# Moving the first input-gate matmul behind the last block of layer 1

## The reference

```python
xn = layernorm(x)
# attention branch (Di = 512, K = 64, R = 16)
u     = xn @ up_w.T                                   # [T, Di]
shift = silu(causal_conv4(u) + conv_b)
v     = sigmoid(u @ ig_w1.T @ ig_w2.T + ig_b2) * u    # the input gate
q, k  = shift @ q_w.T, shift @ k_w.T
g     = softplus(shift @ g_w.T + g_b);  tau = sigmoid(shift @ tau_w.T + tau_b)
o     = gla_chunk_scan(q, k_normed * g**tau, v, -g * tau)
o     = rmsnorm((o + shift * residual_weight) * silu(xn @ gate_w.T)) @ down_w.T
# feed-forward branch (D_HID = 1024, ternary weights with a scale per output)
h = silu(w1(xn)) * w2(xn)                             # layer 1
h = gelu(h1(h)); h = gelu(h2(h)); y = w3(h)
out = x + o + y
```

## Time and profile before

| | us |
|---|---|
| median of 3 runs | 2048.26 (2047.7 to 2049.34) |
| profiled execution, its own time | 2048.48 |
| span of the profiled execution | 2046.7 |
| TensorE busy in it | 1989.6 (97%) |
| VectorE busy | 1576.1 (77%) |
| ScalarE busy | 1260.1 (62%) |

### The profile page before, as it was taken

How to read it: one execution, slowest core, us unless ns; L and a number is a source line. 1 busy time by engine, 2 the same in 40 slices (tenths; PEclk the granted TensorE clock), 3 DMA queues, 4 the chain that set the end, 5 groups by cost and what they waited for, 6 DMA issues and landing times.

```text
span 2046.7 us, 46221 instructions
## 1 busy us (share of the span) xinstructions
PE 1989.6 (97%) x17218; PEld 1966.2 (96%) x17218; DVE 1576.1 (77%) x4242; ACT 1260.1 (62%) x2495; POOL 68.5 (3%) x104
## 2 busy tenths in 40 slices
PE   0999999999999999999999999999999999999998
PEld 0999999999999999999999999999999999999998
DVE  7777778877777877787777788777778777878776
ACT  5665656666566666566656566665566665666564
POOL 0000000000000000000000000000000000000000
PEclk9999999999999999999999999999999999999999
DMA  8000000000000000000000000000000000000000
GB/s 292 7 12 12 11 7 6 12 12 12 12 1 12 12 12 12 12 1 12 11 12 11 7 6 12 12 12 12 1 11 12 12 12 12 1 12 11 12 7 7
DMA packets 23359, 34.18 MB, mean 17 GB/s; under 512 B 2946, under 2 KB 19714, under 8 KB 23187
## 3 DMA queue, kind: packets, MB, share of 16 engines
q1 hardware_dynamic: 23186, 31.46, 4.6%
HBM read 23.07 MB, written 8.39 MB: 15 GB/s over the span
## 4 chain that ended last, share of the span: by engine, by line
PE 85%; DVE 5%; issue 5%; ACT 4%; SPq 1%; DMA 0%; DVEq 0%; POOLq 0%; POOL 0%; ACTq 0%
PE fb L355 56%; PE ab L355 23%; PE ab L523 2%; ACT raw L754 1%; PE ab L479 1%; PE ab L467 1%; PE ab L405 1%; ACT L747 1%; PE fb L601 1%; ACT hid0h L672 1%; DVE work L1009 0%; DVE raw L904 0%; DVE v L963 0%; ACT hid1h L672 0%; DVE att L980 0%
## 5 line engine op out<-in xcount | busy, mean ns | idle before, releaser
L355 PE MATMUL fb<-hid1h,wwhole 128*128 128x256 f32 x2048 | 492.8, 283 | 4.3 <-DVE hid1l L807 1.0
L355 PE MATMUL fb<-hid1l,wwhole 128*128 128x256 f32 x2048 | 485.1, 279 | 0.0
L355 PE MATMUL fb<-hid0h,wwhole 128*128 128x256 f32 x2048 | 483.8, 279 | 0.0
L355 PE MATMUL fb<-hid0l,wwhole 128*128 128x256 f32 x2048 | 483.8, 279 | 0.0
L355 PEld LDWEIGHTS fb<-hid1h,wwhole 128*128 128x128 f32 x2048 | 384.2, 188 | 11.9 <-issue 8.9
L355 PEld LDWEIGHTS fb<-hid1l,wwhole 128*128 128x128 f32 x2048 | 384.4, 188 | 0.0
L355 PEld LDWEIGHTS fb<-hid0l,wwhole 128*128 128x128 f32 x2048 | 384.2, 188 | 0.0
L355 PEld LDWEIGHTS fb<-hid0h,wwhole 128*128 128x128 f32 x2048 | 384.1, 188 | 0.0
L754 ACT ACTIVATE raw<-fb,sh_s 128x256 f32<-128x256 f32 x512 | 213.1, 467 | 207.9 <-PE fb L355 207.0
L355 PE MATMUL fb<-xnth,wwhole 128*128 128x256 f32 x1024 | 239.3, 277 | 0.0
L355 PE MATMUL fb<-xntl,wwhole 128*128 128x256 f32 x1024 | 239.1, 277 | 0.0
(11 more groups left out here) (206 smaller groups left out, 4570.2 us busy)
## 6 DMA issues: line engine op xcount, KB each, us to landing
xin<-x SPq DMA_DIRECT2D x32, 256.0 KB, 2.7
out<-xin SPq DMA_DIRECT2D x32, 256.0 KB, 2.2
stage_more<-stage_w SPq DMA_DIRECT2D x6, 512.0 KB, 7.3
sgate<-stage_w SPq DMA_DIRECT2D x4, 512.0 KB, 4.1
shift<-stage_w SPq DMA_DIRECT2D x4, 512.0 KB, 4.9
v<-stage_w SPq DMA_DIRECT2D x4, 512.0 KB, 5.3
raw<-stage_w SPq DMA_DIRECT2D x3, 512.0 KB, 6.1
mixed<-stage_w SPq DMA_DIRECT2D x3, 512.0 KB, 8.5
```

What stands on the lines that cost most here:

```text
L355: mm = pe.matmul(o, a, b, start=start and i == 0, stop=stop and i == len(pairs) - 1)
```

## The change

```diff
                 for m in range(4, FB):
-                    if m == FB - 2:
-                        pe.wait_ge(gate_ev.sem, gate_ev.at(me, 1))
-                        input_gate(0)
                     layer1(m)
+                pe.wait_ge(gate_ev.sem, gate_ev.at(me, 1))
+                input_gate(0)
                 input_gate(1)
```

## The result

The changed kernel takes 2057.88 us (median of 6 runs, 2056.71 to 2058.83) against 2048.95 us of the kernel before in the same series (6 runs): a ratio of 1.0044, 95% interval 1.0034 to 1.0054, so 7 to 11 us slower. The forecast was 7.2 us and 2055.5 us, in a range of 2051.5 to 2060. The profiled execution took 2056.71 us, its span is 2054.9, 8.2 us more than before.

The account below looks back on a forecast made before the run. TensorE bounds the kernel, with a stop in h2 fed by a slackless ScalarE-VectorE chain. Tanh delays of 2.9 us (p = 0) and 4.3 us (p = 1) sum to 7.2 us: 2055.5 us, range 2051.5 to 2060.

Parts of the forecast that it names:

- The bound and the chain: TensorE 97% busy, stopping about 0.3 us at h2's 13th matmul; a delayed tanh delays it equally through ScalarE and VectorE.
- rival of a hidden slack: VectorE's wait for silu(5) or the h2 stop has another cause, so the delay vanishes: 2048.3 us, chance 0.05.
- rival of TensorE's order: Posed for the experiments: the loss comes from TensorE's new order, not ScalarE's queue; no chance given.
- When TensorE issues the matmul: First input-gate matmul starts 1.81 us later, after sixteen matmuls at 0.1132 us; tanh late by 0.19 (p = 0), 0.27 us (p = 1).
- What TensorE wins or loses: From the second input-gate matmul on, TensorE's stream is unmoved; projections stay covered by 0.5 us; nothing saved.
- The sum: 15 halves at 0.19 us and 16 at 0.27 us give 7.2 us; the first half counts nothing.
- The pace behind the stop: Rival: h2 matmuls behind the stop turn fast in 9 to 31 halves, leaving the loss within 0.2%; chance 0.08.
- More matmuls of h2 at 0.113 us: Sign of a wrong forecast: more of h2's matmuls running at the fast pace than before.
- The rule of the Trainium skill: Full-clock gap of 0.109 us per 256-column matmul; sixteen take 1.75 us, giving a 5.2 us sum and 2053.5 us.

Follow-up runs that it names:

- e1: The changed kernel with ScalarE's silu(5) moved ahead of the first tanh and hid0(1) behind it: 2040.89 us, 0.9964 of the kernel before.
- e4: The kernel before with one added, unused 128x128 copy on ScalarE ahead of the first tanh in every half: 2055.91 us, ratio 1.0039.
- e2: The kernel before with ScalarE's silu(5) moved ahead of the first tanh and hid0(1) behind it: 2038.27 us, ratio 0.9956.

## Why the prediction was right

**The bound and the chain** held. The one misreading is of size: of the 31 waits in the earlier trace rows 30 are about 0.3 us, and the one booked on `hid1h`, in the first half of the last sequence, is 0.9 us. The stop at the 13th matmul of h2 is ended by `hid1l`; e1 removes it by an edit on ScalarE's queue and e4 enlarges it by another, with TensorE's program unchanged. The rival of a hidden slack is out, and so is the rival of TensorE's order: e4 gives the loss without it.

**When TensorE issues the matmul.** I chose the fast pace for blocks 6 and 7. From the third half on the matmul starts at 13.39 us into the half as forecast, and the tanh at 13.83 as forecast for p = 0 (316.61 - 302.78) and within 0.01 for p = 1.

**What TensorE wins or loses.** Nothing, as worked out: projections at 14.94 us as before, but for the first two halves.

**The sum.** 7.2 us were forecast for the stops of 31 halves; 7.6 were read. The extra comes from two halves that the forecast took as the others: the stop of the second grew by 0.42 us and that of the first half of the last sequence by 0.47. The term that was wrong is the first half's: "its delay is hidden to about its own slack and I count nothing". In the two traces it cost about a microsecond. ScalarE of the kernel before, then TensorE of the same, in the first half:

```profile
68.19 0.60 ACT L694 ACTIVATE work<-ab 128x512 f32<-128x512 f32 x1
```

```profile
66.78 0.40 PE L467 MATMUL ab<-ig2s,zs 81*128 81x512 f32 x1
```

And ScalarE and TensorE of the changed kernel:

```profile
69.31 0.60 ACT L693 ACTIVATE work<-ab 128x512 f32<-128x512 f32 x1 [0.80 <-PE ab L467]
```

```profile
92.86 0.35 PE L355 MATMUL fb<-hid1h,wwhole 128*128 128x256 f32 x1 [0.68 <-DVE hid1l L806]
```

The matmul's end and the tanh lay only 68.19 - 67.18 = 1.01 us apart there, against 1.66 us in a later half (316.42 - 314.76). Sixteen matmuls at the slow pace, 1.89 us, explain 0.9 us of the delay (1.89 - 1.01 + 0.04). The first input-gate matmul was later by another 0.16 us, since TensorE had been slower ahead of block 6. Counted from the start of the half, the tanh came 1.09 us late instead of 0.2. That this half had no stop of its own I took for room, and it had about 0.2 us: the changed kernel waits 0.68 us there, its 13th matmul of h2 is 0.90 us later, and the half is 1.1 us longer. The total of this half is the least certain number here, since its first third differs by more than a microsecond between traces with the same program on TensorE (the projections start 16.35 us into it in e2, 17.67 in the kernel before).

**The pace behind the stop**, the rival with 0.08, came partly true: 10 halves instead of 4 at the fast pace, where 9 more were needed to bring the loss under 0.2%. I had not looked at w3, where the same switch went the other way. Both together moved the total by -0.9 us. That the change caused either switch was not shown. More matmuls of h2 at 0.113 us had been named as a sign of a wrong forecast; the sign appeared, in 6 more halves where 9 were needed.

**Luck.** That 7.2 us lie so near the 8.2 us of the traces is in part luck: 1.1 us of the first half were left out, and the pace, left out as well, took 0.9 us back. The medians differ by 8.9 us.

**The rule of the Trainium skill** ("TensorE: Matmul & The Clock Gate", section "Back-to-back issue gap") would have given delays of 0.13 and 0.21 us. Measured: 0.19 and 0.28. The gap of 0.113 us decided, not 0.109.

## What to carry to other kernels

In this kernel a producer moved later on a saturated engine cost little or nothing (0.0009, interval 0.0000 to 0.0018) while it was still done before its consumer's queue reached it; past that point nearly every tenth of a microsecond went through, because the queue behind the consumer feeds a chain without slack. So price such a move by the consumer's queue, not by the engine on which it is made, and look behind the waiting instruction for the one that others wait for: putting that one first took away the loss and the older stop as well. Work it out for the first iteration on its own, since its engines stand differently to each other.

## What the hardware showed that I had not expected

TensorE's stream of weight load and 256-column matmul has two paces, 0.1133 and 0.1178 us, at the same granted clock (1.00 in both stretches), operands and instruction mix. It keeps one over long stretches: in most halves the stream is fast from the start, slow behind the first input-gate matmul, and behind a stop it is one or the other. In h1 it was mostly slow in every kernel here. Not every change of pace stands at a wait or at a matmul of another shape: in w3 of the half that starts at 302.78 us in the kernel before, the distances are 0.118 us up to the 6th matmul, (358.87 - 358.40) / 4, and 0.113 from there on, (361.82 - 358.87) / 26. The shape is the same, and the program waits only before the 1st, 9th, 17th and 25th matmul (rows 2 to 7 and the 32nd):

```profile
358.40 0.28 PE L355 MATMUL fb<-wwhole,hid0l 128*128 128x256 f32 x1
358.51 0.28 PE L355 MATMUL fb<-wwhole,hid0h 128*128 128x256 f32 x1
358.63 0.28 PE L355 MATMUL fb<-wwhole,hid0l 128*128 128x256 f32 x1
358.75 0.28 PE L355 MATMUL fb<-wwhole,hid0h 128*128 128x256 f32 x1
358.87 0.28 PE L355 MATMUL fb<-wwhole,hid0l 128*128 128x256 f32 x1
358.99 0.28 PE L355 MATMUL fb<-wwhole,hid0h 128*128 128x256 f32 x1
...
361.82 0.28 PE L355 MATMUL fb<-wwhole,hid0l 128*128 128x256 f32 x1
```

The difference between the paces is 0.0045 x 256 = 1.15 us a half for h1 and h2 together.
